# Third feed-forward stage: where the residual is scaled and added, and where the rounding factors lie

## The chip, the cores and the metric

The kernel runs on one core of one Trainium2 chip. The metric is the device time of one execution in microseconds (us); the times shown are medians of several executions. PE is TensorE, DVE is VectorE, ACT is ScalarE, POOL is GpSimd.

## The reference, cut to what matters

A tensor `x` of 64 x 64 x 128 numbers passes through four layers, each a cross attention and a feed-forward. The change lies in the third feed-forward and touches how the fourth attention begins:

```python
x = x + tanh(g_ffn[2]) * L2_ffn(layernorm(x), w_fc, b_fc, w_proj, b_proj)

def block_quant(v, m_bits, bk):          # m_bits 3, bk 32, over the last dimension
    amax = max(abs(vb))                  # of each block of 32
    e = floor(log2(maximum(amax, 2.0 ** -126)))
    scale = exp2(e - m_bits)
    return round(vb / scale) * scale
def lowprec_linear(x, w, b):
    return einsum('bsk,nk->bsn', block_quant(x), block_quant(w)) + b
h = gelu(lowprec_linear(x, w_fc, b_fc))  # hidden width 512
return lowprec_linear(h, w_proj, b_proj)
```

## The kernel before, in words

The 4096 rows of `x` stay in SBUF as 32 tiles of 128 x 128 (`x_sb`). Stages follow one another; the third feed-forward (`ffn2` on each engine) works on pairs of tiles, 16 pairs, in a software pipeline whose order is `pair_order`: `step(c, x, h, px, ph)` for c from 0 to 18, where `x` is the pair whose rows are quantised in step c, `px = c - 1` the pair that passes the first product, `h = c - 2` the pair whose hidden values are quantised, and `ph = c - 3` the pair that passes the second product and gets its residual. Steps 0 and 1 are done inside the attention before. Each engine runs its own queue in program order, and semaphores tie them together.

One step in the middle does this:

- **VectorE** takes the largest magnitude of each block of 32 in one instruction over 128 x 1280 (the rows of one pair and the hidden values of another, L1774), masks out its exponent (an int32 AND in place on `e`, L1777), forms the rounding factor `m = max(e, 2^-126) * 1.5 * 2^20` (L1780), and adds `m` to the numbers (L1781, result `q_r`), which rounds them. Then it adds the residual of pair `ph` (two `scalar_tensor_tensor` of 128 x 128 from PSUM, L1636, called from L1784), measures these tiles for the next normalisation (`bn_stats` L1787, `bn_aggr` L1791), and in every second step adds the epsilon for two pairs (`pair_measured`, L1759, between L1774 and L1777).
- **GpSimd** subtracts the factor again (`lower_blocks`, L1278, 128 x 1280, result `q_out` in bf16), and in every second step takes the power -1/2 of four variances (L1294). From step 16 on it also normalises the first tiles for the next attention (`normal_rows`, L1376 and L1378).
- **TensorE** puts the bias of the first product into PSUM (L641) and the bias of the second (L862), keeps its clock up with two products whose result nobody reads (L522), turns the quantised rows (L638) and hidden values (L897), makes the first product (L881) and the second (L886), and works ahead on keys and values for the fourth attention (L528, L537).
- **ScalarE** copies the turned rows (L1049) and hidden values (L1199) from PSUM, normalises the rows of a later pair (L988), applies Gelu to the first product (L1055), which writes the hidden values into the buffer that VectorE quantises in the next step, and keeps the keys and values that were made ahead (L976, L980).

The Gelu of step c waits for VectorE's addition of the same step, since both use the same buffer:

```python
                if px is not None:
                    act.wait_ge(quotients[0], c + 1)
                    hidden2(px)
```

VectorE's reduction of step c waits for that Gelu of step c - 1 (`hid_ready`). GpSimd's subtraction waits for VectorE's addition (`quotients`), and TensorE's transposes of step c wait for GpSimd's subtraction of step c - 1 (`q_ready`). In the last two steps TensorE issues six and twelve clock-keeping products (L522) ahead of its transposes. The outputs of the second product lie in two PSUM banks, one for each tile of the pair.

## Time and profile before

| | us |
|---|---|
| median of 3 runs (lowest, highest) | 1058.82 (1058.22, 1059.3) |
| the profiled execution | 1061.08 |
| its span, first to last instruction | 1059.3 |
| busy: PE, DVE, ACT, POOL | 896.4, 873.2, 679.0, 577.7 |

The span is the stretch in which instructions ran; 1.78 us of the profiled execution lie around it. The steady steps of the stage lie between about 710 and 768 us of the span, its last three steps end at about 782 us, and the fourth attention follows. A row of a timeline gives the start and the duration of an instruction, or of several alike that follow one another (x2 at its end); the brackets tell how long the engine had been idle before it and what released it.

### The profile page before, as it was taken

How to read it: one execution, taken by the hardware profiler on the slowest of the kernel's cores; microseconds unless marked ns; L12 is line 12 of the kernel's file. 1: busy time of each engine (PE TensorE's matmuls, PEld its weight loads, DVE VectorE, ACT ScalarE, POOL GpSimd, SP SyncE). 2: the span in 40 equal slices, each digit the busy share in tenths (PEclk: the TensorE clock that was granted, in tenths of full speed). 3: DMA queues.
4: the chain of work that ended last, by engine and by line, in shares of the span. 5: the costliest groups of instructions: out<-in, count | busy, mean ns of one | idle time of the engine just before them, and what ended most of it. 6: DMA issues, size and time to landing. Idle time of an engine off the chain costs nothing.

```text
span 1059.3 us, 30026 instructions
## 1 busy us (share of the span) xinstructions
PE 896.4 (85%) x11481; PEld 694.4 (66%) x11481; DVE 873.2 (82%) x2299; ACT 679.0 (64%) x1740; POOL 577.7 (55%) x691
## 2 busy tenths in 40 slices
PE   8999999999999963699959999988889999634553
PEld 5888879988887751366638888844458778412232
DVE  5999988878899974256649999869978999799997
ACT  5888864367777730245438888868867788544553
POOL 6444402243457667322178888235553788667644
PEclk9999999999999976799989999969999999755555
DMA  8760000000000011465311111000000000000000
GB/s 223 177 256 3 2 2 2 2 2 3 3 17 27 28 37 52 123 186 150 103 43 35 32 33 33 7 1 1 2 2 3 2 2 3 1 5 16 15 21 25
DMA packets 60527, 44.43 MB, mean 42 GB/s; under 512 B 15196, under 2 KB 55781, under 8 KB 59366
## 3 DMA queue, kind: packets, MB, share of 16 engines
q1 hardware_dynamic: 55718, 34.09, 11.0%
q0 software_dynamic: 4096, 8.34, 2.7%
q8 instruction: 90, 1.47, 0.6%
q14 instruction: 47, 0.39, 0.1%
q10 hardware_dynamic: 576, 0.13, 0.1%
HBM read 23.73 MB, written 18.87 MB: 40 GB/s over the span
## 4 chain that ended last, share of the span: by engine, by line
PE 53%; DVE 19%; POOL 12%; issue 9%; ACT 3%; DMA 2%; DVEq 1%; POOLq 0%; SPq 0%; ACTq 0%
PE ps L777 8%; PE ps L735 8%; PE ps L708 6%; PE ps L618 4%; POOL big L1248 3%; PE ps L749 3%; PE ps L821 3%; PE ps L812 3%; PE ps L813 3%; PE ps L528 3%; DVE rowmax L1976 2%; POOL slots L1264 2%; PE ps L672 2%; PE ps L628 2%; DVE big L1848 2%
## 5 line engine op out<-in xcount | busy, mean ns | idle before, releaser
L1976 DVE TENSOR_REDUCE rowmax<-ps 128x16 f32<-128x1024 f32 x128 | 155.4, 1214 | 25.8 <-PE ps L708 24.8
L1982 DVE TENSOR_TENSOR sm<-ps,rowmax 128x512 f32<-128x512 f32 x256 | 164.9, 686 | 3.4
L1084 ACT ACTIVATE pr<-ps 128x512 f32<-128x512 f32 x256 | 139.0, 595 | 43.7 <-PE ps L777 39.2
L777 PE MATMUL ps<-cst,sm 128*128 128x128 f32 x1024 | 140.2, 277 | 11.6 <-DVE sm L1982 9.2
L735 PE MATMUL ps<-vbd,pr 128*64 128x18 f32 x4096 | 141.6, 212 | 0.6 <-ACT pr L1084 0.5
L735 PEld LDWEIGHTS ps<-vbd,pr 128*64 128x64 f32 x4096 | 133.9, 138 | 5.2 <-ACT pr L1084 1.6
L777 PEld LDWEIGHTS ps<-cst,sm 128*128 128x128 f32 x1024 | 112.4, 141 | 27.0 <-issue 18.5
L1407 POOL TENSOR_SCALAR xn<-x_sb,mv_all,rstd_all 128x128 f32<-128x128 f32 x122 | 97.5, 799 | 35.7 <-PE ps L672 28.5
L963 ACT ACTIVATE qbd<-ps,bqp,cst 128x128 f32<-128x128 f32 x256 | 104.9, 465 | 5.7 <-PE ps L688 1.9
L1248 POOL DMA_INDIRECT big<-expert_out,row_g x64 | 68.6, 1072 | 38.6 <-DMA expert_out<-xn_all 23.0
L1264 POOL DMA_INDIRECT slots<-xn_all,row_s x64 | 65.0, 1015 | 34.4 <-DVE sm L1982 18.2
L1240 POOL TENSOR_TENSOR rstd_all<-mv_all,cst 128x1 f32<-128x1 f32 x64 | 36.1, 567 | 78.2 <-DVE mv_all L1954 37.8
L908 PE MATMUL ps<-wT,xqT_both 128*128 128x512 bf16 x60 | 28.3, 627 | 56.6 <-ACT xqT_both L1049 54.5
L1021 ACT ACTIVATE vbd<-ps 64x128 f32<-64x128 f32 x192 | 53.4, 278 | 24.2 <-PE ps L528 16.0
L1254 POOL TENSOR_TENSOR rstd_all<-mv_all,cst 128x1 f32<-128x1 f32 x60 | 34.5, 574 | 60.4 <-DVE mv_all L1948 51.0
L1278 POOL TENSOR_TENSOR q_out<-q_r,q_s 128x1280 bf16<-128x1280 f32 (+2 forms) x18 | 37.9, 2105 | 49.8 <-DVE q_r L1781 43.4
L1098 ACT ACTIVATE oT<-ps 128x128 f32<-128x128 f32 x128 | 35.5, 278 | 45.0 <-PE ps L681 44.0
L1636 DVE SCALAR_TENSOR_TENSOR x_sb<-ps,tg,x_sb 128x128 f32<-128x128 f32 x192 | 54.6, 289 | 11.4 <-PE ps L886 7.6
L2095 DVE TENSOR_TENSOR pr<-ps,pr 128x512 f32<-128x512 f32 x32 | 22.0, 691 | 50.4 <-ACT pr L1151 50.2
L749 PE MATMUL ps<-wo,oT 128*128 128x128 f32 x256 | 61.6, 323 | 1.4 <-ACT oT L1098 1.4
L528 PE MATMUL ps<-wv,ctxT 128*64 128x64 f32 x1024 | 53.7, 235 | 2.1 <-ACT big L976 2.0
L1474 POOL TENSOR_TENSOR hid<-sm 128x512 f32<-128x512 f32 x16 | 22.7, 1421 | 59.9 <-DMA sm<-slots 59.9
(314 smaller groups left out, 2356.2 us busy)
## 6 DMA issues: line engine op xcount, KB each, us to landing
slots<-hT SPq DMA_DIRECT2D x8, 1024.0 KB, 11.9
sm<-slots SPq DMA_DIRECT2D x32, 256.0 KB, 3.1
expert_out<-xn_all SPq DMA_DIRECT2D x16, 256.0 KB, 3.0
ew<-in_L_ffn_w SPq DMA_DIRECT2D x24, 128.0 KB, 2.6
out<-x_sb SPq DMA_DIRECT2D x32, 64.0 KB, 1.5
slots<-xn_all,row_s POOLq DMA_INDIRECT x64
big<-expert_out,row_g POOLq DMA_INDIRECT x64, 2.7
x_sb<-in_x SPq DMA_DIRECT2D x1, 512.0 KB, 4.5
```

The lines of the kernel that those rows point to most:

```text
L528: last = nc.tensor.matmul(dst[a * S:(a + 1) * S, b * S:(b + 1) * S].rearrange("p (r w) -> p r w", r=RG), ctxT[:, t * P + b * S:t * P + (b ...
L708: last = nc.tensor.matmul(bank(0, r)[:, b * P:(b + 1) * P], qbd[x][rows, b * S:(b + 1) * S, :].rearrange("d q h -> d (q h)"), keys[rows, : ...
L735: last = nc.tensor.matmul(dst[:, :, h2, :], probs[:, h2, :], heads[:, :, h2, :], start=True, stop=True, skip_group_check=True)
L749: last = nc.tensor.matmul(mixed[:, M_Y], oT[x][:, :], wo[l][:, :], start=True, stop=(l != 2))
L777: last = nc.tensor.transpose(turned[b][:, r * P:(r + 1) * P], sm[x][:, c:c + P], ident)
L963: last = nc.scalar.activation(qbd[y][:, :, a], src[:, P:2 * P], ACT.Identity, scale=parity[:, a:a + 1], bias=bqp[l][:, a:a + 1])
L1084: nc.scalar.activation(pr[y][:, b, :], turned[b], ACT.Exp, scale=SCALE).then_inc(p_ready[y], 1)
L1248: nc.gpsimd.indirect_dma_start(got[i % 2][s][:, k, :], None, eo_d, bass.IndirectOffsetOnAxis(ap=row_g[:, k, t:t + 1].bitcast(U32), axis=0) ...
L1264: nc.gpsimd.indirect_dma_start(slots_d[c], bass.IndirectOffsetOnAxis(ap=row_s[:, c, u:u + 1].bitcast(U32), axis=0), xn_all[:, u * D:(u + 1 ...
L1407: nc.gpsimd.tensor_scalar(xn[buf][:, :], xt, mv_all[:, 2 * u:2 * u + 1], rstd_all[:, u:u + 1], ALU.subtract, ALU.mult).then_inc(xn_ready[b ...
L1976: v.tensor_reduce(row3, sc, AX.X, ALU.max).then_inc(rowmax_ready[x], 1)
L1982: v.tensor_tensor(sm[x][:, :].rearrange("p (r g k) -> p r g k", r=RG, k=S)[:, part], sc[:, part], row3[:, part].unsqueeze(3).broadcast_to( ...
```

## The change

The residual of pairs 0 to 14 no longer goes through VectorE. In the step after the second product, ScalarE multiplies both tiles of the pair by the gate from PSUM into SBUF (`scale_outputs`, the first instruction of its step), and GpSimd adds the result to `x_sb` behind its subtraction of that step (one addition of 128 x 256). VectorE measures the pair one step later than GpSimd adds it, two steps after the product, so `pair_measured` and the power on GpSimd move by two pairs as well. The last pair keeps VectorE's residual; two pairs are measured behind it. Both tiles of the second product now share one bank (`both_y`), and its bias is put there behind the first product instead of ahead of the transposes. From step 2 on VectorE writes the rounding factors into PSUM and reads them there; GpSimd forms its own copy in SBUF from the exponents. VectorE's wait for GpSimd's last subtraction moves from the factor to the addition.

```diff
@@ names, beside the other PSUM views
         outputs = bank(1, 3)[:, P:(1 + NS) * P].rearrange("p (s d) -> p s d", s=NS)
         fp4_ps = bank(1, 2)[:, 0:3 * (HW // Q16)].rearrange("p (n b) -> p n b", n=3)
+        both_y = bank(0, 3)[:, P:(1 + NS) * P]
+        factors = bank(1, 3)[:, 3 * P:3 * P + QMAX // Q32]
+        scaled_y = [hid[p][:, 0:NS * D] for p in range(2)]
+        ADDED = IT - 1
+        BLOCK_STEPS, BLOCK_WEIGHT_STEPS = 3, 4
@@ TensorE, ffn2
                         lift_bias(s)
-                    if ph is not None:
-                        pe.wait_ge(x_done[s], IT * FFN2 + ph)
-                        nc.tensor.matmul(bank(s, 3)[:, P:2 * P], ones_b[0:3, :], bias3[:, F2:F2 + D], start=True, stop=False, skip_group_check=True)
...
                 if ph is not None:
+                    if 1 <= ph <= ADDED:
+                        pe.wait_ge(y_scaled, ph)
                     for s in range(NS):
+                        if ph == 0 or ph > ADDED:
+                            pe.wait_ge(x_done[s], IT * FFN2 + ph)
+                        nc.tensor.matmul(both_y[:, s * D:(s + 1) * D], ones_b[0:3, :], bias3[:, F2:F2 + D], start=True, stop=False, skip_group_check=True)
                         pe.wait_ge(hqT_ready[s], ph + 1)
                         for n in range(4):
-                            last = nc.tensor.matmul(bank(s, 3)[:, P:2 * P], hqT[s][:, n * P:(n + 1) * P], wT[:, 1, n * P:(n + 1) * P],
+                            last = nc.tensor.matmul(both_y[:, s * D:(s + 1) * D], hqT[s][:, n * P:(n + 1) * P], wT[:, 1, n * P:(n + 1) * P],
@@ ScalarE
+            def scale_outputs(i):
+                for s in range(NS):
+                    act.wait_ge(y_ready[s], IT * FFN2 + i + 1)
+                if i > 1:
+                    act.wait_ge(x_done[0], IT * FFN2 + i - 1)
+                nc.scalar.activation(scaled_y[i % 2], both_y, ACT.Copy, scale=tg[:, 6:7]).then_inc(y_scaled, 1)
+
             def ffn2(c, x, h, px, ph):
                 if c < 2:
                     return
+                if ph is not None and 1 <= ph <= ADDED:
+                    scale_outputs(ph - 1)
                 if px is not None:
                     empty_quantised(FFN2, px)
@@ GpSimd, lower_blocks
                     span = both_sides(x, h)
+                    if c > 1:
+                        blk = slice(span.start // Q32, span.stop // Q32)
+                        pool.wait_ge(quant_step[0], BLOCK_WEIGHT_STEPS + BLOCK_STEPS * c + 2)
+                        pool.wait_ge(q_ready[0], c)
+                        nc.gpsimd.tensor_scalar(q_s[:, 1, blk], q_s[:, 0, blk], 2.0 ** -126, 1.5 * 2.0 ** 20, ALU.max, ALU.mult).then_inc(factors_kept, 1)
+                        pool.wait_ge(factors_kept, c - 1)
                     pool.wait_ge(quotients[0], c + 1)
...
                 if c >= IT:
                     normal_rows(3, c - IT)
-                if ph is not None and ph % 2 == 1:
-                    pool.wait_ge(mv_ready[0], IT * FFN2 + ph + 1)
...
+                if ph is not None and 1 <= ph <= ADDED:
+                    xt = x_sb[:, (ph - 1) * NS * D:ph * NS * D]
+                    pool.wait_ge(y_scaled, ph)
+                    nc.gpsimd.tensor_tensor(xt, scaled_y[(ph - 1) % 2], xt, ALU.add).then_inc(x_done[0], 1)
+                    pool.wait_ge(x_done[0], IT * FFN2 + ph)
+                    pool.sem_inc(x_done[1], 1)
+                if ph is not None:
+                    for i in (ph - 2, ph) if ph == IT - 1 else (ph - 2,):
+                        if i > 0 and i % 2 == 1:
+                            pool.wait_ge(mv_ready[0], IT * FFN2 + i + 1)
...
@@ VectorE, ffn2
-                    src, e, m = q_in[:, span], q_s[:, 0, blk], q_s[:, 1, blk]
+                    src, e, m = q_in[:, span], q_s[:, 0, blk], factors[:, blk] if c > 1 else q_s[:, 1, blk]
+                    if c > 2:
+                        dve.wait_ge(factors_kept, c - 2)
                     link(v.tensor_reduce(e, blocks(src, Q32), AX.X, ALU.max, apply_absolute_value=True))
-                    if ph is not None and ph > 0 and ph % 2 == 0:
-                        pair_measured(ph - 1)
+                    if ph is not None and ph > 2 and ph % 2 == 0:
+                        pair_measured(ph - 3)
                     link(v.tensor_scalar(e.bitcast(I32), e.bitcast(I32), EXPONENT, None, ALU.bitwise_and))
-                    if c > 0:
+                    if c == 1:
+                        dve.wait_ge(q_ready[0], 1)
+                    link(v.tensor_scalar(m, e, 2.0 ** -126, 1.5 * 2.0 ** 20, ALU.max, ALU.mult))
+                    if c > 1:
                         dve.wait_ge(q_ready[0], c)
-                    link(v.tensor_scalar(m, e, 2.0 ** -126, 1.5 * 2.0 ** 20, ALU.max, ALU.mult))
                     v.tensor_tensor(blocks(q_r[:, span], Q32), blocks(src, Q32), over(m, Q32), ALU.add).then_inc(quotients[0], 1)
-                if ph is not None:
+                if ph is not None and ph > 1:
+                    measured(ph - 2)
+                if ph == IT - 1:
+                    pair_measured(ph - 2)
                     for s in range(NS):
-                        residual(FFN2, ph, s, tg[:, 6:7], s)
-                    dve.drain()
+                        dve.wait_ge(y_ready[s], IT * FFN2 + ph + 1)
+                        dve.wait_ge(x_done[s], IT * FFN2 + ph)
                     for s in range(NS):
-                        v.bn_stats(bst[s][:, :], x_sb[:, (ph * NS + s) * D:(ph * NS + s + 1) * D])
-                    dve.drain()
-                    for s in range(NS):
-                        u = ph * NS + s
-                        v.bn_aggr(mv_all[:, 2 * u:2 * u + 2], bst[s][:, :]).then_inc(aggr_ready[s], 1)
-                    if ph == IT - 1:
-                        pair_measured(ph)
+                        t = ph * NS + s
+                        xt = x_sb[:, t * D:(t + 1) * D]
+                        v.scalar_tensor_tensor(xt, both_y[:, s * D:(s + 1) * D], tg[:, 6:7], xt, ALU.mult, ALU.add).then_inc(x_done[s], 1)
+                    measured(ph - 1)
+                    measured(ph)
+                    pair_measured(ph)
+
+            def measured(i):
+                for s in range(NS):
+                    dve.wait_ge(x_done[s], IT * FFN2 + i + 1)
+                    dve.wait_ge(aggr_ready[s], IT * FFN2 + i)
+                    v.bn_stats(bst[s][:, :], x_sb[:, (i * NS + s) * D:(i * NS + s + 1) * D])
+                dve.drain()
+                for s in range(NS):
+                    u = i * NS + s
+                    v.bn_aggr(mv_all[:, 2 * u:2 * u + 2], bst[s][:, :]).then_inc(aggr_ready[s], 1)
```

## Rows read from the trace of the kernel before

**Rows 1.** Busy time by stretch: us, each engine busy (instructions), PEclk, DMA, GB/s.

```profile
700.00:709.90 9.90, 8.06 (x61) 5.15 (x62) 4.67 (x10) 5.66 (x12) 3.63 (x2) 0.55 0.00 0
714.75:763.30 48.55, 43.26 (x431) 20.93 (x430) 45.58 (x107) 40.52 (x86) 28.46 (x16) 1.00 0.00 1
```

**Rows 2.** Timeline, two middle steps: start, us, engine, line, operation [idle before <-releaser].

```profile
737.81 2.35 POOL L1278 TENSOR_TENSOR q_out<-q_r,q_s 128x1280 bf16<-128x1280 f32 x1 [0.83 <-DVE q_r L1781]
...
739.07 1.45 DVE L1774 TENSOR_REDUCE q_s<-hT 128x40 f32<-128x1280 f32 x1
...
740.55 0.18 DVE L1777 TENSOR_SCALAR q_s<-q_s 128x40 int32<-128x40 int32 x1
740.60 0.38 ACT L1049 ACTIVATE xqT_both<-ps 128x256 bf16<-128x256 bf16 x1 [0.41 <-PE ps L638]
...
740.99 1.49 DVE L1781 TENSOR_TENSOR q_r<-hT,q_s 128x1280 f32<-128x1280 f32 x1
...
742.40 0.60 DVE L1636 SCALAR_TENSOR_TENSOR x_sb<-ps,tg,x_sb 128x128 f32<-128x128 f32 x2
742.56 2.35 POOL L1278 TENSOR_TENSOR q_out<-q_r,q_s 128x1280 bf16<-128x1280 f32 x1 [2.40 <-DVE q_r L1781]
742.60 1.09 ACT L1055 ACTIVATE hT<-ps 128x512 f32<-128x512 f32 x2
743.09 0.49 DVE L1787 BATCH_NORM_STATS2 bst<-x_sb 128x6 f32<-128x128 f32 x2
...
743.82 1.46 DVE L1774 TENSOR_REDUCE q_s<-hT 128x40 f32<-128x1280 f32 x1
...
745.37 0.17 DVE L1759 TENSOR_SCALAR mv_all<-mv_all 128x4 f32<-128x4 f32 x1
...
745.95 1.49 DVE L1781 TENSOR_TENSOR q_r<-hT,q_s 128x1280 f32<-128x1280 f32 x1
```

**Rows 3.** Timeline around the sixteenth quantisation, GpSimd and VectorE.

```profile
773.06 0.80 POOL L1376 TENSOR_SCALAR xn<-x_sb,mv_all,rstd_all 128x128 f32<-128x128 f32 x1
773.83 0.45 POOL L1378 TENSOR_TENSOR x_sb<-x_sb,y_bias_b 128x128 f32<-128x128 f32 x1
...
774.03 0.28 DVE L1759 TENSOR_SCALAR mv_all<-mv_all 128x4 f32<-128x4 f32 x1
...
774.64 1.23 DVE L1781 TENSOR_TENSOR q_r<-hT,q_s 128x1024 f32<-128x1024 f32 x1
```

**Rows 4.** All instances of two lines: count, duration ns min/median/max, first and last start.

```profile
L1848 DVE SCALAR_TENSOR_TENSOR big<-big x30: 628/684/2186, 928.2 to 1045.7; 128x512 f32<-128x512 f32 x30
...
L1617 DVE TENSOR_SCALAR q_m<-xn_all x1: 952/952/952, 492.7 to 492.7; 128x1536 int32<-128x1536 int32 x1
```

**Rows 5.** Sizes on GpSimd and VectorE: single lines (as rows 4), one group.

```profile
L1428 POOL TENSOR_TENSOR x_sb<-x_sb,y_bias_b x87: 452/458/472, 13.5 to 894.4; 128x128 f32<-128x128 f32 x87
...
L1278 POOL TENSOR_TENSOR big<-big 128x512 f32<-128x512 f32 x30 | 31.1, 1057 | 31.4 <-DVE big L1852 30.5 <-DVE big L1829 0.7
...
L1294 POOL TENSOR_TENSOR rstd_all<-mv_all,cst x8: 1006/1006/1040, 716.5 to 782.9; 128x4 f32<-128x4 f32 x8
...
L1828 DVE TENSOR_SCALAR ps<-big x16: 228/228/228, 922.6 to 1042.7; 128x64 f32<-128x64 f32 x16
```

**Rows 6.** Timeline of ScalarE and VectorE at the start of the steady stretch.

```profile
708.38 1.08 ACT L1055 ACTIVATE hT<-ps 128x512 f32<-128x512 f32 x2
709.80 1.45 ACT L976 ACTIVATE big<-ps,bkp,odd_pair 128x512 f32<-128x512 f32 x2 [0.35 <-PE ps L537]
...
709.94 1.45 DVE L1774 TENSOR_REDUCE q_s<-hT 128x40 f32<-128x1280 f32 x1
```

**Rows 7.** Timeline of the stage's end (columns as rows 2).

```profile
775.95 1.91 POOL L1278 TENSOR_TENSOR q_out<-q_r,q_s 128x1024 bf16<-128x1024 f32 x1 [0.45 <-DVE q_r L1781]
...
780.68 0.84 DVE L1636 SCALAR_TENSOR_TENSOR x_sb<-ps,tg,x_sb 128x128 f32<-128x128 f32 x2 [3.25 <-PE ps L886]
...
782.69 1.23 DVE L1976 TENSOR_REDUCE rowmax<-ps 128x16 f32<-128x1024 f32 x1
```

12 lines of the change are left out of this document (6 added, 6 removed).

## The prediction, made before the changed kernel ran

> **What bounds the kernel now.** I read first the busy time by stretch, to see what the stage of the change is limited by, then the timeline of two middle steps, to find the loop behind that limit, and last the timelines of the stage's two ends. In the steady stretch VectorE is busy 45.58 of 48.55 us, TensorE 43.26, ScalarE 40.52, GpSimd 28.46 [rows 1]. Ten steps fill it, so one takes 4.856 us. VectorE looks like the bound, and the change takes work off it. But the timeline shows three loops of almost the same length [rows 2].
>
> First, VectorE's own queue. From one reduction to the next it is 743.82 - 739.07 = 4.75 us, and 0.21 more where the pair's epsilon is added (745.95 - 743.82 = 2.13 from reduction to addition, against 740.99 - 739.07 = 1.92): 4.75 and 4.96, mean 4.856.
>
> Second, the loop through Gelu. It starts about 0.04 after the addition, takes 1.09, and the reduction can follow by 0.12 (742.60 + 1.09 = 743.69 against 743.82, so 0.12 is an upper bound). Then come 1.92 to the addition and its 1.49: 0.04 + 1.09 + 0.12 + 1.92 + 1.49 = 4.66, with the epsilon 4.87, mean 4.77.
>
> Third, a loop over two steps through GpSimd. Addition's end to subtraction 0.08 (740.99 + 1.49 = 742.48, 742.56); subtraction 2.35; its end to ScalarE's copy 0.44 (737.81 + 2.35 = 740.16, 740.60); copy to Gelu 2.00 (742.60); then 1.09, 0.12, 2.13 and 1.49. Sum 9.70, or 4.85 a step, against 4.856 measured. ScalarE sits idle 0.41 before the copy in this parity, so the lateness comes from GpSimd.
>
> So VectorE, if it lost all that the change removes, would still wait for Gelu, and Gelu for GpSimd.
>
> **What is removed.** VectorE's two residuals go: 743.09 - 742.40 = 0.69 a step [rows 2]. Nothing is late any more on VectorE by itself, and next comes Gelu. By the third loop the gain is at most 4.856 - 4.85, practically 0 a step. The reduction is unchanged; moving the wait for the subtraction from the factor to the addition gains nothing, since the subtraction ends 2.43 after the addition (0.08 + 2.35) and the factor comes later than that. The measuring stays (0.49 and about 0.25) but fits in the 1.25 until Gelu's end. In the first two steps with an output nothing is measured yet.
>
> **ScalarE's scaling.** 128 x 256 from PSUM: a bf16 copy of that width took 0.38, and two Gelus of 512 took 1.09, some 0.55 each [rows 2]; I take 0.42 between 0.38 and 0.55. It comes ahead of the copy, into an idle 0.41 in the tight parity; consecutive instructions of ScalarE overlap by some 0.1 (two of 0.6 in 1.09), so it is just covered: 0, at most 0.1 a step. If this cover were gone, 0.4 a step would go onto the third loop. TensorE's next output product waits for this scaling, but it stands behind the copies that ScalarE does after it. The bias product moves from an idle spell before the transposes into the wait for the copied hidden values: 0.
>
> **Factors in PSUM.** The nearest row that writes PSUM from a small tile is 0.228 for 64 columns [rows 5], against 0.18 for 40 columns in SBUF [rows 2]. I take 0.02 a step, bounds 0 and 0.05. The addition reads one operand from PSUM instead of SBUF; nothing in its 1280 columns changes: 0. GpSimd's own copy of the factors, 128 x 40, is under its 128 x 128 addition of 0.46 [rows 5]; I take 0.35. It runs while VectorE forms the factor and adds (1.7 us), so it is covered, also behind a power of 1.01.
>
> **GpSimd's addition and what it blocks.** This decides the steady part. A two-input addition of 128 columns takes 0.458 and a two-input operation of 512 takes 1.057 [rows 5]; in line, 256 columns take 0.66 (bounds 0.55 and 0.80). It stands right behind the subtraction, so it lasts from 2.43 to 3.08 after VectorE's addition ended. In the same count VectorE's reduction ends at 0.04 + 1.09 + 0.12 + 1.48 = 2.73. The next instruction is the AND in SBUF, or the epsilon. What happens when such a short VectorE instruction meets a GpSimd one shows once: the epsilon at 774.03 took 0.28 instead of the 0.17 of 745.37, and ended at 774.31, while GpSimd's 128 x 128 addition ended at 774.28 [rows 2, 3]. The larger meetings have the same pattern: L1848 has a median of 0.684 and a longest of 2.186 [rows 4]. And the AND is of the kind that runs at two columns a cycle: 1536 int32 columns took 0.952, so 0.62 ns each [rows 4], where the addition takes 1.49 for 1280. So I take it that the AND (or the epsilon) cannot begin until GpSimd's addition has ended, at 3.08, and ends at 3.11.
>
> The Trainium skill has this as a rule ("SBUF — State Buffer", Who interferes with whom): VectorE and GpSimd share a pair of ports that one of them holds for a whole instruction, and a `tensor_scalar` with SBUF on both sides can ask for it. The trace agrees in the 0.28 above. Without the rule the steady part would come out at 0 instead of the +0.4 below. The page "VectorE: DVE Perf Modes" (Why PSUM operands drop a tier) says that a PSUM operand keeps an instruction out of the two-port mode, so by it the factor into PSUM would not be held; no row here shows such a meeting.
>
> The step then goes: AND ends 3.11, factor at 3.15, addition 0.22 + 0.02 later, 1.49: 4.88. With the epsilon: it ends 3.11, the addition starts 774.64 - 774.31 = 0.33 later [rows 3], plus 0.02 and 1.49: 4.95. Mean 4.91, against 4.856: +0.05 a step, over ten steps (from the fourth addition, where the first pair is added, to step 15) +0.5. With a 0.55 addition the third loop holds and this is 0; with 0.80 it is +0.19 a step, +1.9.
>
> **The start.** The reduction at 709.94 came behind residual and measuring; Gelu had ended at 708.38 + 1.08 = 709.46, so it can come 0.36 sooner [rows 6]. But ScalarE was busy until 709.80 + 1.45 = 711.25, and the scaling now stands between that and the copy, without an idle spell: later by 0.3 to 0.4. Of the 0.36 I keep 0.2 as a gain; bounds -0.6 and +0.3.
>
> **The end.** Here GpSimd's queue is the path. Before, its last subtraction started at 775.95 and took 1.91 [rows 7], two normalisations and bias additions followed (0.80 + 0.45 each, less overlap 1.22, as at 773.06 [rows 3]), and it was done by 780.3. VectorE's last residual came at 780.68 and ended at 781.52, and the attention's first row maximum at 782.69 [rows 7], 1.17 later. New: the blocked additions in steps 16 and 17 cost some 0.35; GpSimd then does, from 773.45 on, rows 1.22, an addition 0.66, the power 1.01, the factors 0.35 (776.7), subtraction 1.91 (778.6), rows 1.22, addition 0.66, rows 1.22, addition 0.66: 782.4. VectorE's last residual now waits for that addition, since it needs `x_done` of the pair before. Two tiles take 0.60, and then two pairs are measured instead of one: 1.17 + 0.75 (743.82 - 743.09 = 0.73 [rows 2]). The row maximum comes at 782.4 + 0.1 + 0.6 + 1.9 = 785.0: +2.3. It carries over in full, since the attention's chain of waits runs through that row maximum. TensorE's transposes of the last hidden values (about 778.9) are just not reached by the late subtraction. Bounds: GpSimd on time and only the second measuring, +0.75; everything late, +2.8.
>
> **Sum.** Start -0.2, steady +0.5, end +2.3: +2.6. The profiled execution would go from 1061.08 to 1063.7; it stands 2.26 above the median, so the median goes from 1058.82 to 1061.4.
>
> **Rivals.**
> - *No hold.* The AND goes past GpSimd's addition. Against it the 0.28 [rows 3]; for it that this is one meeting of another operation. Steady 0, and GpSimd's queue at the end loses only the 0.35: -0.2 + 0 + 1.9 = +1.7, 1060.5. Chance 0.15.
> - *The clock falls.* TensorE would be idle from its last output product (about 781) to 783.1 and again for 1.8, where it now waits half a microsecond. In 700 to 709.9 it was granted 0.55 [rows 1], that is, mostly 1.2 GHz instead of 2.4, behind a handover with idle spells. In the fourth attention TensorE is nearly always busy, so an estimate is that 7 us at half clock, less the time it idles anyway, lose some 3: 2.6 + 3.0 = +5.6, 1064.4. Against it: the attention begins with clock-keeping products. Chance 0.2.
> - *Faster.* VectorE's relief shows: Gelu's loop at 4.77 would be the limit if ScalarE came to its Gelu sooner than the third loop says, -0.09 for 13 steps, -1.1; the start gives its whole 0.6; and GpSimd reaches its last addition before TensorE's last output (by 780.7), so that only the second measuring less TensorE's 0.4 from the moved bias is added: +0.35. Sum -1.4, 1057.4. It is decided by GpSimd's last addition: every 0.1 by which it ends after 780.7 goes onto the time. Against it: that sum of queued work ends 1.7 later. Chance 0.1.
> - *The sum above*, with its spread, 0.55.
>
> **The numbers.** About 0.2% (2.1 us) is what a measurement of this kernel can tell from no change. The sum at +2.6 is slower; with its bounds one part in four falls below 2.1. No hold is mostly "same", the clock "slower", the faster rival mostly "same". Slower is 0.55 x 0.75 = 0.41, 0.20 from the clock and 0.01 from no hold, 0.62; the faster rival gives 0.07 to faster and 0.03 to same; the rest is same, 0.31. The range takes from -0.8 (half of the faster rival) to +5.7 (the clock, or long GpSimd additions).
>
> **What would show it.** Steady steps of 4.86 to 4.95, with L1777 or L1759 at 0.4 to 0.5 us instead of 0.18, ending just behind GpSimd's addition. VectorE idle for about 0.5 before each reduction, released by Gelu. The last residual released by GpSimd's addition, and the row maximum 4.3 us behind the last output product instead of 1.5. It is wrong if the steady step falls under 4.8, if the AND stays at 0.18 under a running GpSimd addition, or if the last residual is released by TensorE.

## The result, and the profile after

The changed kernel took 1064.30 us (median of 8 runs, 1062.74 to 1068.29), the kernel before 1058.78 beside it (8 runs, 1057.81 to 1061.27). The ratio is 1.0053, with an interval of 1.0043 to 1.0064: slower by 5.5 us. The profiled execution took 1063.8 us, its span is 1062.0.

To see where the time came from I took the starts of VectorE's reductions in the stage from the timeline, and those of the first row maxima of the attention behind it. "Start" runs from the third reduction to the sixth, "steady" over the ten steps from there, "end" from the sixteenth reduction to the first row maximum, "first step" from there to the second. What lies ahead of the stage and behind it is the same code.

| us | start | steady | end | first step | sum against before |
|---|---|---|---|---|---|
| before | 18.81 | 48.56 | 19.44 | 3.98 | |
| after | 18.99 | 49.98 | 22.39 | 4.70 | +5.3 |

The four stretches together lose 5.3, close to the 5.5 of the timing. They come from one profiled execution each, and outside them the two executions differ where their code doesn't: the one of before reaches the third reduction 2.1 later (695.88 against 693.76) and takes 0.4 longer behind the last stretch, so that the profiled executions as wholes differ by 2.7 only. The steady stretch first, two steps of after in the timeline (columns as [rows 2], where two steps of before stand):

```profile
732.41 1.49 DVE L1806 TENSOR_REDUCE q_s<-hT 128x40 f32<-128x1280 f32 x1 [0.49 <-issue]
733.99 0.41 DVE L1789 TENSOR_SCALAR mv_all<-mv_all 128x4 f32<-128x4 f32 x1
...
734.76 1.49 DVE L1815 TENSOR_TENSOR q_r<-hT,ps 128x1280 f32<-128x1280 f32 x1
...
737.46 1.49 DVE L1806 TENSOR_REDUCE q_s<-hT 128x40 f32<-128x1280 f32 x1 [0.49 <-issue]
738.98 0.48 DVE L1809 TENSOR_SCALAR q_s<-q_s 128x40 int32<-128x40 int32 x1
...
731.24 1.09 ACT L1063 ACTIVATE hT<-ps 128x512 f32<-128x512 f32 x2
...
733.65 0.73 POOL L1318 TENSOR_TENSOR x_sb<-hid,x_sb 128x256 f32<-128x256 f32 x1
...
...
738.69 0.73 POOL L1318 TENSOR_TENSOR x_sb<-hid,x_sb 128x256 f32<-128x256 f32 x1
...
759.00 0.73 POOL L1318 TENSOR_TENSOR x_sb<-hid,x_sb 128x256 f32<-128x256 f32 x1
759.04 0.73 DVE L1809 TENSOR_SCALAR q_s<-q_s 128x40 int32<-128x40 int32 x1
```

VectorE now idles 0.49 before most reductions, as its residuals are gone. The profile names no releaser for it ("issue"), but the reduction starts 0.08 after Gelu's end (731.24 + 1.09 = 732.33, 732.41). GpSimd's addition ends at 733.65 + 0.73 = 734.38 and the epsilon at 734.40; the next one ends at 739.42 and the AND at 739.46. Before, they took 0.17 and 0.18 [rows 2]. So in nine of the ten steps one of the two is held until GpSimd's addition ends, in one of them by only 0.03. A step mostly takes 4.97 from reduction to reduction where the AND is held, 5.04 where the epsilon is, against 4.75 and 4.96. Two of the ten are longer. In the last of the rows above the AND is held for GpSimd's whole addition, since the subtraction ahead of it had started 0.24 later than elsewhere; that step takes 5.22. Another takes 5.18, and the one behind it only 4.86; the experiments come back to it. The first of the ten is a control within the kernel:

```profile
714.28 0.18 DVE L1809 TENSOR_SCALAR q_s<-q_s 128x40 int32<-128x40 int32 x1
...
713.10 0.74 POOL L1318 TENSOR_TENSOR x_sb<-hid,x_sb 128x256 f32<-128x256 f32 x1
```

There GpSimd's addition has ended at 713.84, the AND takes its 0.18, and the step takes 4.67 (712.76 to 717.43).

By groups of the same stretch, GpSimd, VectorE and ScalarE (count, busy us and mean ns of one):

```profile
L1318 POOL TENSOR_TENSOR x_sb<-hid,x_sb 128x256 f32<-128x256 f32 x10 | 7.3, 730 | 0.0
L1184 ACT ACTIVATE hid<-ps,tg 128x256 f32<-128x256 f32 x10 | 4.8, 481 | 0.0
...
L1809 DVE TENSOR_SCALAR q_s<-q_s 128x40 int32<-128x40 int32 x10 | 3.5, 355 | 0.2
L1305 POOL TENSOR_SCALAR q_s<-q_s 128x40 f32<-128x40 f32 x10 | 3.5, 348 | 3.0 <-DVE q_s L1809 2.0 <-POOL rstd_all L1325 1.0
L1812 DVE TENSOR_SCALAR ps<-q_s 128x40 f32<-128x40 f32 x10 | 2.0, 203 | 0.3
L1789 DVE TENSOR_SCALAR mv_all<-mv_all 128x4 f32<-128x4 f32 x4 | 1.4, 356 | 0.4
```

The start, ScalarE and GpSimd in after's timeline. It answers to [rows 6]:

```profile
707.87 1.45 ACT L984 ACTIVATE big<-ps,bkp,odd_pair 128x512 f32<-128x512 f32 x2 [0.92 <-PE ps L543]
709.21 0.47 ACT L1184 ACTIVATE hid<-ps,tg 128x256 f32<-128x256 f32 x1
709.57 0.39 ACT L1057 ACTIVATE xqT_both<-ps 128x256 bf16<-128x256 bf16 x1
...
710.80 2.35 POOL L1295 TENSOR_TENSOR q_out<-q_r,q_s 128x1280 bf16<-128x1280 f32 x1 [1.61 <-PE ps L884]
```

The scaling stands in ScalarE's full queue, the copy behind it is late, and with it TensorE's first product (L884). GpSimd's subtraction, which by the program waits for that product (`h_psum`), idles 1.61 until it, and the next reduction comes 5.72 behind the one before (707.04 to 712.76), where before it was 4.75. The step ahead of that had gained 0.79 (8.60 against 9.39). How much falls to which of the two varies between executions in which this code is the same (8.79 and 5.57, 8.79 and 5.53 in two kernels below), while their sum stays at 14.32 to 14.36, against 14.14 before.

The end, VectorE, GpSimd and TensorE. It answers to [rows 7]:

```profile
782.69 0.61 DVE L1826 SCALAR_TENSOR_TENSOR x_sb<-ps,tg,x_sb 128x128 f32<-128x128 f32 x2 [1.21 <-POOLq L1320]
...
785.13 1.22 DVE L2022 TENSOR_REDUCE rowmax<-ps 128x16 f32<-128x1024 f32 x1
...
779.62 0.72 POOL L1318 TENSOR_TENSOR x_sb<-hid,x_sb 128x256 f32<-128x256 f32 x1
780.61 0.80 POOL L1407 TENSOR_SCALAR xn<-x_sb,mv_all,rstd_all 128x128 f32<-128x128 f32 x1 [0.28 <-POOL x_sb L1318]
...
781.78 0.72 POOL L1318 TENSOR_TENSOR x_sb<-hid,x_sb 128x256 f32<-128x256 f32 x1
...
780.19 0.40 PE L894 MATMUL ps<-wT,hqT 128*128 128x128 bf16 x4
783.40 1.24 PE L714 MATMUL ps<-big,qbd 32*128 32x128 f32 x16 [2.81 <-DVE x_sb L1826]
```

GpSimd is the path here: its last addition ends at 782.50 and releases the last residual, two pairs are measured behind it, and the row maximum follows 2.44 after the residual's start. TensorE is idle for 2.81 meanwhile. What that does to its clock is in the busy time by stretch (columns as [rows 1]):

```profile
781.92:788.75 6.83, 5.35 (x31) 3.75 (x32) 4.63 (x14) 1.60 (x5) 4.79 (x7) 0.50 0.00 0
```

From 781.92 to 788.75 it was granted half, 1.2 GHz, just where the attention begins; the kernel before had the full 2.4 GHz there. The attention's first step took 4.70 instead of 3.98. Its busy time in before and then in after:

```profile
782.69:786.67 3.98, 3.10 (x32) 1.88 (x30) 2.51 (x4) 2.46 (x7) 3.45 (x5) 1.00 0.00 0
```

```profile
785.13:789.82 4.69, 4.69 (x32) 2.99 (x32) 2.51 (x4) 2.46 (x7) 3.44 (x5) 0.61 0.00 0
```

The same 32 products fill the whole step now, where they had left 0.88 of it free.

### The profile page after: what moved, and what is told of

Read it like the earlier page. It is cut to its first block, busy times and chain, and to the rows that moved or that the text cites. A ratio compares the mean times of both kernels' runs of the same rounds, so it can differ in the third digit from the quotient of the medians.

```text
span 1062.0 us, 30107 instructions
## 1 busy us (share of the span) xinstructions
PE 895.1 (84%) x11481; PEld 695.1 (65%) x11481; DVE 868.5 (82%) x2269; ACT 685.1 (65%) x1755; POOL 595.9 (56%) x722
## 4 chain that ended last, share of the span: by engine, by line
PE 53%; DVE 16%; POOL 14%; issue 10%; ACT 4%; DMA 2%; POOLq 0%; SPq 0%; DVEq 0%; ACTq 0%
PE ps L783 9%; PE ps L741 8%; PE ps L714 6%; PE ps L624 4%; POOL big L1265 3%; POOL q_out L1295 3%; PE ps L755 3%; PE ps L827 3%; PE ps L818 3%; PE ps L819 3%; PE ps L534 2%; DVE rowmax L2022 2%; POOL slots L1281 2%; PE ps L678 2%; PE ps L634 2%
## 5 line engine op out<-in xcount | busy, mean ns | idle before, releaser
L916 PEld LDWEIGHTS ps<-wT,xqT_both 128*128 128x128 bf16 x60 | 6.5, 130 | 68.4 <-ACT xqT_both L1057 57.9
```

## The experiments

Twelve kernels, each timed beside the kernel before on its own chip. The profiled executions give the four stretches; the ratio is the timed one. Four of them (AND from PSUM, end repaired, clock kept, bank and factors) ran on a chip where the kernel before takes 1075.45 us; the instructions of the stage take as long there.

| kernel | start | steady | end | first step | sum against before | ratio (interval) |
|---|---|---|---|---|---|---|
| AND from PSUM | 18.73 | 49.19 | 22.24 | 4.82 | +4.2 | 1.0033 (1.0020 to 1.0047) |
| half the addition | 19.02 | 48.90 | 21.40 | 4.19 | +2.7 | 1.0021 (1.0010 to 1.0032) |
| scaling alone | 19.24 | 48.88 | 19.45 | 3.99 | +0.8 | 0.9995 (0.9985 to 1.0005) |
| end repaired | 19.04 | 49.98 | 19.64 | 3.98 | +1.9 | 1.0012 (1.0000 to 1.0024) |
| clock kept | 18.99 | 49.96 | 22.39 | 3.98 | +4.5 | 1.0041 (1.0026 to 1.0056) |
| bank and factors | 19.29 | 49.71 | 19.35 | 3.99 | +1.6 | 1.0009 (0.9996 to 1.0022) |
| bank only | 19.34 | 51.18 | 19.33 | 3.98 | +3.0 | 1.0036 (1.0023 to 1.0049) |
| epsilon later | 19.01 | 57.00 | 24.46 | 3.98 | +13.7 | 1.0113 (1.0098 to 1.0128) |
| epsilon later, end repaired | 19.23 | 57.03 | 22.01 | 3.98 | +11.5 | 1.0118 (1.0103 to 1.0132) |
| epsilon earlier | 18.85 | 55.14 | 22.03 | 3.98 | +9.2 | 1.0059 (1.0044 to 1.0075) |
| the same, rows first | 19.00 | 53.92 | 19.23 | 3.98 | +5.3 | 1.0046 (1.0033 to 1.0059) |
| before, rows first | 18.97 | 48.69 | 19.44 | 3.98 | +0.3 | 1.0007 (0.9998 to 1.0017) |

The ten steady steps are numbered one to ten below.

### The hold: AND from PSUM, and half the addition

```diff
-link(v.tensor_reduce(e, blocks(src, Q32), ...))
+top = tops[:, blk] if c > 1 else e          # tops lies in PSUM
+link(v.tensor_reduce(top, blocks(src, Q32), ...))
-link(v.tensor_scalar(e.bitcast(I32), e.bitcast(I32), EXPONENT, None, ALU.bitwise_and))
+link(v.tensor_scalar(e.bitcast(I32), top.bitcast(I32), EXPONENT, None, ALU.bitwise_and))
```

> The changed kernel, but from step 2 on VectorE's reduction writes the block maxima into PSUM and the AND reads them there (its result still goes to SBUF), so that no form of the AND has SBUF on both sides. Theory (the AND is held by GpSimd's addition): L1777's successor is back from 0.48 to about 0.20 us in every second step although GpSimd's addition is running, the other steps stay held through the epsilon; the ten steady steps go from 49.98 us to about 49.0, the total falls by about 1.0 from 1064.3. Rival (the steady steps are long because ScalarE's scaling delays the copy and Gelu, or because of the PSUM operand of the addition): the AND is shorter, but the steps stay at 49.8 to 50.0 us.

VectorE and GpSimd in its timeline:

```profile
743.62 0.20 DVE L1811 TENSOR_SCALAR q_s<-ps 128x40 int32<-128x40 int32 x1
...
743.32 0.73 POOL L1319 TENSOR_TENSOR x_sb<-hid,x_sb 128x256 f32<-128x256 f32 x1
```

GpSimd's addition runs until 744.05. The AND, which now reads PSUM, begins and ends under it. The steady stretch went from 49.98 to 49.19.

```diff
-nc.gpsimd.tensor_tensor(xt, scaled_y[(ph - 1) % 2], xt, ALU.add)
+nc.gpsimd.tensor_tensor(xt[:, 0:D], scaled_y[(ph - 1) % 2][:, 0:D], xt[:, 0:D], ALU.add)
```

> The kernel after with GpSimd's residual addition cut to 128x128 (0.46 us instead of 0.73); the second tile of each pair doesn't get its residual, the rest is unchanged. Ten steady steps took 48.56 us before and 49.98 after. Hold theory (the AND or epsilon waits until GpSimd's addition has ended): the addition ends 0.27 earlier, about where VectorE's reduction ends, so the AND takes 0.18 to 0.25 again and the ten steps take 49.0 to 49.3 us, as in the kernel whose AND reads PSUM (49.19). Rival, that the addition itself lengthens GpSimd's queue and so the loop through Gelu: it would also help the other kernel's remainder, 48.6 to 48.9. Rival, that the addition's size does not matter: 49.9 to 50.0. End of the stage (last-but-two reduction to first row maximum) 22.39 after: about 0.5 to 0.8 less here, 21.6 to 21.9.

This kernel leaves out the second tile's residual. 48.90 lies on the edge between the hold's range and that of the rival which blames GpSimd's longer queue, so by itself it can't tell them apart, and the end took 21.40, below the 21.6 that I had set as its least; the groups of its steady stretch show that the meeting is gone:

```profile
L1809 DVE TENSOR_SCALAR q_s<-q_s 128x40 int32<-128x40 int32 x10 | 2.0, 198 | 0.2
L1789 DVE TENSOR_SCALAR mv_all<-mv_all 128x4 f32<-128x4 f32 x4 | 0.7, 171 | 0.4
```

The AND is back from 355 ns to 198 and the epsilon from 356 to 171. Of the 1.42 us that after lost in the steady stretch, 0.8 come back in the one way and 1.1 in the other; I take the hold to be that much. It is less than the 2.2 us by which those instructions had grown (3.5 + 1.4 against 2.0 + 0.7), so a second limit stands close behind: both kernels mostly go at 4.86 to 4.90 a step. What it is shows in where Gelu starts. In a step without an epsilon of the kernel with half the addition:

```profile
727.10 2.35 POOL L1295 TENSOR_TENSOR q_out<-q_r,q_s 128x1280 bf16<-128x1280 f32 x1 [0.27 <-POOL q_s L1305]
...
729.89 0.38 ACT L1057 ACTIVATE xqT_both<-ps 128x256 bf16<-128x256 bf16 x1
...
730.17 1.49 DVE L1815 TENSOR_TENSOR q_r<-hT,ps 128x1280 f32<-128x1280 f32 x1
731.89 1.08 ACT L1063 ACTIVATE hT<-ps 128x512 f32<-128x512 f32 x2
```

Gelu starts 0.23 after the addition's end (731.66, 731.89). It comes 2.00 after ScalarE's copy, and the copy 0.44 after the subtraction's end (729.45, 729.89): the same 0.44 and 2.00 as in the prediction's third loop. In the steps with an epsilon Gelu follows the addition by 0.03, and the step is the loop through Gelu with the epsilon in it, 4.86 to 4.87 as the prediction counted it. So VectorE's relief ends at two limits that both lie at what before took on the average, 4.856.

### What remains: ScalarE's scaling

```diff
+if ph is not None and ph >= 1:
+    for s in range(NS):
+        act.wait_ge(x_done[s], IT * FFN2 + ph)
+    nc.scalar.activation(hid[ph % 2][:, 0:NS * D], x_sb[:, (ph - 1) * NS * D:ph * NS * D], ACT.Copy, scale=tg[:, 6:7])
```

> The kernel before, with a 128x256 scaling added on ScalarE ahead of each step's copy (its result goes nowhere); nothing else is moved. Theory that ScalarE's scaling is covered by the idle 0.41 before the copy in the tight parity: ten steady steps 48.5 to 48.7 us as before (48.56). Rival, that it is part of the third loop (GpSimd's subtraction to ScalarE's copy to Gelu): every second step is later by 0.1 to 0.5, ten steps 49.0 to 50.0, and the remainder of 0.63 that the kernel with the AND from PSUM leaves is ScalarE's. At the start (third to sixth reduction, 18.81 before) both expect 0.2 to 0.6 more.

This stand-in reads `x_sb` in SBUF and waits for VectorE's residual; it takes 0.54, not 0.48. Put into the kernel before, it costs 0.32 in the steady stretch and 0.43 at the start. Neither range had the 0.32. Of the ten steps nine are as before within 0.04, so there the scaling is covered. One, the sixth, takes 5.02 where it was 4.75:

```profile
741.49 0.28 PE L638 MATMUL ps<-ident_b,q_out 128*128 128x128 bf16 x2 [0.33 <-POOL q_out L1282]
...
742.16 0.38 ACT L1049 ACTIVATE xqT_both<-ps 128x256 bf16<-128x256 bf16 x1 [0.30 <-issue]
```

ScalarE's copy starts 0.39 after the transposes' end there, and 0.10 in every other step; the profile names nothing that it waits for. All nine kernels with a scaling ahead of that copy have this gap in the sixth step and in no other of the ten (0.39, in three of them 0.55), and the three with neither the scaling nor another order on ScalarE have 0.10 in all ten. What it is stays open. It is the 5.18 of after, where the next step gives 0.18 of it back, since the addition then just misses the epsilon, and most of what the kernel with half the addition has over before (0.34). In the changed kernel the scaling so costs next to nothing net in the steady stretch. The timing (0.5 us faster, 1.6 faster to 0.5 slower) doesn't confirm the 0.8 of the profiled executions, so a cost of this size is read from the trace, not timed.

### The end and the clock

```diff
 # GpSimd, per step
-if c >= IT:
-    normal_rows(3, c - IT)
 (the addition of the pair before)
+if c in (IT - 3, IT - 1, IT + 2):
+    normal_rows(3, {IT - 3: 0, IT - 1: 1, IT + 2: 2}[c])
 # VectorE, last step
 pair_measured(ph - 2)
+measured(ph - 1)
 (waits for output and x_done, last residual)
-measured(ph - 1)
 measured(ph)
```

> The changed kernel with another order at the end alone: GpSimd normalises the attention's tiles 0 and 1 in steps 13 and 15, and tile 2 behind its last addition, and VectorE measures pair 14 ahead of its wait for the last output. Theory (the end is GpSimd's queue plus the second measuring): from the last full reduction (step 15) to the attention's first row maximum 22.4 us becomes 19.7 to 20.4, and the total falls by 2 to 2.7 from 1064.3; the last residual is released by TensorE again. In steps 13 to 15 the AND or the epsilon may be held once more, up to +0.5. Rival (the end is long through TensorE, its clock or its transposes): 22 us or more stays, total 1064.

VectorE and GpSimd at the end of it:

```profile
796.66 0.61 DVE L1827 SCALAR_TENSOR_TENSOR x_sb<-ps,tg,x_sb 128x128 f32<-128x128 f32 x2
...
798.26 1.23 DVE L2022 TENSOR_REDUCE rowmax<-ps 128x16 f32<-128x1024 f32 x1
...
793.98 0.72 POOL L1316 TENSOR_TENSOR x_sb<-hid,x_sb 128x256 f32<-128x256 f32 x1
794.88 0.73 POOL L1316 TENSOR_TENSOR x_sb<-hid,x_sb 128x256 f32<-128x256 f32 x1 [0.17 <-ACT hid L1184]
```

GpSimd's last addition now ends at 795.61, one microsecond ahead of the residual, and only one pair is measured behind it (1.60 from residual to row maximum instead of 2.44). The residual waits for nobody: VectorE comes to it straight from measuring the pair before, not released by TensorE as I had expected. The end takes 19.64, just under the 19.7 to 20.4 and 2.75 less than after, and the clock doesn't fall, which brings 0.72 more. That is 3.5 us of the 5.3; the ratio falls from 1.0053 to 1.0012.

```diff
 pair_order(pe, ffn2)
+pe.wait_ge(ahead_kept, 2 * GROUPS)
+keep_clock(12)
 attention(3)
```

> The changed kernel plus twelve clock-keeping products on TensorE between its last output product and the attention's first scores. Theory (the wait there costs the clock, and the clock costs about 0.7 us): the granted clock stays 1.0 at 782 to 789, the second row maximum follows the first after 4.0 us instead of 4.69, the total falls by 0.5 to 1.0 from 1064.3, everything ahead of the first row maximum stays. Rival (the clock costs the 3 us of the prediction's estimate): the total falls by 2 or more. Other rival (it falls for another cause): no difference in granted clock.

Busy time by stretch of this kernel, up to the first row maximum and the attention's first step behind it:

```profile
781.00:803.20 22.20, 20.54 (x178) 10.99 (x178) 14.25 (x42) 13.98 (x31) 18.43 (x21) 1.00 0.01 1
803.22:807.20 3.98, 2.44 (x28) 1.58 (x27) 2.52 (x4) 1.81 (x5) 3.43 (x5) 1.00 0.00 0
```

With products in TensorE's gap the clock stays at full and the first step takes 3.98, while the end stays 22.39. So the fallen clock cost 0.72 us, by the trace; the two ratios, 1.0053 and 1.0041, have intervals that overlap. Until the first row maximum TensorE's slow products cost nothing.

### Both outputs in one bank, and the factors in PSUM

First the kernel after without its scaling and without GpSimd's addition: VectorE adds and measures every pair in its own step as before, out of the one bank, and the factors stay in PSUM with GpSimd's copy beside them.

```diff
-scale_outputs(ph - 1)                                # ScalarE
-nc.gpsimd.tensor_tensor(xt, scaled_y[...], xt, ALU.add)
-measured(ph - 2)                                     # VectorE
+v.scalar_tensor_tensor(xt, both_y[:, s * D:(s + 1) * D], tg[:, 6:7], xt, ALU.mult, ALU.add).then_inc(x_done[s], 1)
+measured(ph)
```

Then the kernel before with the bank alone, in which VectorE also waits for both outputs before its first residual:

```diff
-pe.wait_ge(x_done[s], IT * FFN2 + ph)                 # early in the step, one bank for each s
-nc.tensor.matmul(bank(s, 3)[:, P:2 * P], ones_b[0:3, :], bias3[:, F2:F2 + D], start=True, ...)
 ...
+for s in range(NS):                                   # behind the first product
+    pe.wait_ge(x_done[s], IT * FFN2 + ph)
+for s in range(NS):
+    nc.tensor.matmul(both_y[:, s * D:(s + 1) * D], ones_b[0:3, :], bias3[:, F2:F2 + D], start=True, ...)
```

> Of the change only the bank shared by both outputs with the bias behind the first product, and the factors in PSUM with GpSimd's own copy; the residual of every pair is VectorE's as before, and no scaling and no addition on GpSimd. Theory (these parts are nearly free): ten steady steps 48.6 to 49.0 us against 48.56 before, the end 19.2 to 19.6 against 19.44, the total 1058.5 to 1059.5. Rival (the PSUM factors or the shared bank carry part of the loss): steady steps above 49.5.

> The kernel before, with both outputs in one bank and the bias product moved behind the first product, in front of the output's own; factors, residual and everything else as before. It splits the kernel that had one bank and the factors in PSUM (ten steady steps 49.71 us against 48.56 before). Theory that the later bias and the wait for both outputs make VectorE's residual late in every second step: 49.1 to 49.7 here. Rival, that the factors in PSUM and GpSimd's factor copy cost it: 48.5 to 48.8 here.

My first expectation was a miss: 49.71, and not 48.6 to 49.0. VectorE's timeline of that kernel:

```profile
755.66 1.49 DVE L1803 TENSOR_TENSOR q_r<-hT,ps 128x1280 f32<-128x1280 f32 x1
757.52 0.61 DVE L1810 SCALAR_TENSOR_TENSOR x_sb<-ps,tg,x_sb 128x128 f32<-128x128 f32 x2 [0.38 <-PE ps L892]
```

The addition ends at 757.15 and the residual waits 0.38 for the output product. That is so in the steps without an epsilon, which take 5.08 instead of 4.75; those with one take 4.86 instead of 4.96 (from the fourth step on). The kernel with the bank alone loses no less: eight of its steps have a mean of 5.02. So the bank, the later bias and the wait for both outputs together cost 0.12 to 0.16 a step on the average where the residual is added in the same step, and some 0.5 at the start (19.29 and 19.34 against 18.81); for a cost of the factors in PSUM nothing is left. One thing does go with the factors: GpSimd starts its subtraction 0.13 to 0.14 after VectorE's addition in this kernel and in after, and 0.08 in before and with the bank alone. In the changed kernel I take the bank's cost to be hidden, since nobody needs the output before the next step; no run here changes the bank alone in it. The 51.18 also holds two long steps, 5.28 and 5.75, 1.0 above the others. What made the first I don't know; in the second TensorE was granted half:

```profile
730.45:733.87 3.42, 3.42 (x42) 2.46 (x42) 2.35 (x7) 2.32 (x6) 2.23 (x1) 0.50 0.00 0
```

### Three places for the epsilon

The epsilon is added between reduction and AND, in the loop through Gelu. I tried to take it off. First behind the step's addition:

```diff
-if ph is not None and ph > 2 and ph % 2 == 0:       # between reduction and AND
-    pair_measured(ph - 3)
 v.tensor_tensor(... over(m, Q32), ALU.add).then_inc(quotients[0], 1)
+if ph is not None and ph > 2 and ph % 2 == 0:
+    pair_measured(ph - 3)
```

> The kernel after, whose reduction leaves the block maxima in PSUM so that the AND reads them there (as in the earlier run, 49.19 for ten steady steps), and whose pair epsilon stands behind the step's addition instead of between reduction and AND. Theory that what remains of 0.63 over before is the epsilon still held in every second step (0.41 instead of 0.17) and its place on the chain: ten steps 48.3 to 48.7. Rival, that the remainder is the longer third loop (scaling on ScalarE, factor copy on GpSimd): 49.0 to 49.2, since the epsilon is then in slack.

> All three repairs of the changed kernel together: AND from PSUM, epsilon behind the addition, and the end with the normal rows of the first tiles earlier and one pair measured ahead of the last wait (the run of that alone: end 19.64 us instead of 22.39, first attention step 3.98 instead of 4.70, ratio 1.0012). If the costs are independent they add: steady 48.3 to 48.7, end 19.6 to 19.7, clock kept, start 18.9 to 19.1; in sum 0.0 to +0.4 us against before, ratio 0.9995 to 1.0005. If the remainder of the steady part belongs to the third loop: steady 49.0 to 49.2, ratio 1.0003 to 1.0010.

Both were far off: 57.00 and 57.03 instead of 48.3 to 49.2. GpSimd in the timeline of the first, in a step at full clock:

```profile
762.82 1.03 POOL L1326 TENSOR_TENSOR rstd_all<-mv_all,cst 128x4 f32<-128x4 f32 x1 [2.16 <-DVE mv_all L1790]
...
764.54 2.35 POOL L1296 TENSOR_TENSOR q_out<-q_r,q_s 128x1280 bf16<-128x1280 f32 x1
```

The power stands in GpSimd's queue ahead of the factor copy and the subtraction. It now waits 2.16 for the epsilon, and the subtraction starts 1.94 after VectorE's addition has ended (761.11 + 1.49 = 762.60), where it had started 0.13 after it. The next reduction waits for the factor copy too, 1.20. Such a step takes 5.47 and the one behind it 5.92. A part of the 57.00 is not the queue's alone: TensorE was granted half from 731.3 to 741.6 and again for some 3 us from 755 on, 0.87 in the mean of the ten steps in both kernels, and the longest step, 7.21, lies there. I had looked at who waits for the epsilon, and not at what is queued behind the one who waits. The second time the epsilon went forward, right behind the pair's measuring, into VectorE's idle time:

```diff
 if ph is not None and ph > 1:
     measured(ph - 2)
+    if ph % 2 == 1:
+        pair_measured(ph - 2)
```

> The changed kernel with the AND reading PSUM, the end repaired (normal rows earlier, one pair measured ahead of the last wait), and the pair's epsilon moved forward, right behind that pair's measuring into VectorE's idle time ahead of the next reduction (the run that moved it back behind the addition was 8 us slower over ten steps, because GpSimd's power waits for it ahead of its factor copy and subtraction). Theory that in the kernel with the AND from PSUM (49.19) every second step was limited by GpSimd's queue (subtraction, addition, power, factor copy: 5.09 from subtraction to subtraction) together with the epsilon on VectorE's chain: 48.2 to 48.9. Rival, that the epsilon is in slack: 49.1 to 49.2. Rival, that it was all the chain: 47.5 to 48.0. End as in the run of that repair alone, 19.4 to 19.7, first attention step 3.98. In sum -0.2 to +0.6 us against before.

55.14, a miss again, and for another reason. VectorE and GpSimd:

```profile
746.31 2.01 DVE L1790 TENSOR_SCALAR mv_all<-mv_all 128x4 f32<-128x4 f32 x1
748.23 1.48 DVE L1808 TENSOR_REDUCE ps<-hT 128x40 f32<-128x1280 f32 x1
...
745.95 2.35 POOL L1296 TENSOR_TENSOR q_out<-q_r,q_s 128x1280 bf16<-128x1280 f32 x1 [1.82 <-PE ps L885]
```

That idle time lies under GpSimd's subtraction. An epsilon on four columns, 0.17 when nothing meets it, took 2.01 and ended at 748.32, as the subtraction ended at 748.30; elsewhere it took 1.65 or 1.66, and a step 5.91. It is the clearest row for the hold in the whole study. TensorE's clock was at half for 10 us within the ten steps and for 7 more at the end, and the end took 22.03. That the late steps made it fall isn't shown: the next kernel has steps of 5.91 as well, and its clock stayed full:

```profile
731.97:742.20 10.23, 9.86 (x70) 5.81 (x72) 7.83 (x15) 6.84 (x15) 6.47 (x6) 0.50 0.01 2
```

### The loop through GpSimd and ScalarE

```diff
+if c + 1 < IT:
+    rows2(c + 1)
 if px is not None:
     empty_quantised(FFN2, px)
 ...
-if c + 1 < IT:
-    rows2(c + 1)
```

> The same kernel, with ScalarE's two normalised rows of the next step moved ahead of its copy of the transposed input, into the idle time in which it waits for TensorE's transposes; Gelu then comes 0.9 us sooner behind that copy. Theory that the loop through GpSimd's subtraction, ScalarE's copy and Gelu holds the steps once VectorE's queue has been relieved: ten steps 47.4 to 48.2 us. Rival, that GpSimd's own queue or VectorE's chain through Gelu holds them: no less than the kernel without this move. In sum against before -1.2 to -0.3 us if the theory holds.

> The kernel before with only that move of the two normalised rows ahead of the copy. Theory that before VectorE's own queue (4.856 a step) is the bound and the loop through GpSimd just its equal: ten steps 48.3 to 48.6 us, no change that the timing could show. Rival, that the loop through GpSimd is the true bound of before: 47.7 or less, and then the change's relief of VectorE was not needed for the gain.

The steady stretch took 53.92, so the range was missed: this kernel still has the early epsilon. Where that is out of the way one sees what the loop allows:

```profile
734.11 1.48 DVE L1808 TENSOR_REDUCE ps<-hT 128x40 f32<-128x1280 f32 x1
...
738.79 1.49 DVE L1808 TENSOR_REDUCE ps<-hT 128x40 f32<-128x1280 f32 x1 [0.49 <-issue]
```

4.68 for the step without an epsilon: its Gelu follows 0.02 behind VectorE's addition, so that is the loop through Gelu alone. But the kernel without this move has steps of 4.68 too. The move does what it was meant to where ScalarE had come late: in most of the steps in which Gelu had started 0.22 or 0.23 after the addition, it starts 0.03 after it. No gain shows, since the reduction behind is held up by the early epsilon. Of the three steps of 6.2 to 6.3 in the kernel without the move one lies within the stretch at half clock and one begins at its end. So the 1.2 us between the two kernels may be the clock's, and what the rows' place is worth is not shown. The control is clear: in the kernel before, the same move gives 48.69 against 48.56, 0.1 above the range that I had given, and a ratio of 1.0007. There VectorE's own queue was the bound, as read.

Not tried was the combination that these runs point to: the epsilon where the change has it, the AND from PSUM, the end repaired, with and without the rows first. Without them, the stretches measured one by one would be 18.9, 49.19, 19.64 and 3.98, by that estimate 0.9 us above before. No kernel in this study beat the one before.

## Why the prediction was right, and where it was off

The time forecast was 1061.4, slower than 1058.82; it came to 1064.30. The loss, 5.5, is over twice the 2.6 of the sum, and it lies 0.2 inside a range that had been drawn as wide for a fallen clock priced four times too high. So the range held in part by luck. The direction and the mechanisms of the hold and of the end held, the three terms of the sum were too small, and one rival came true beside it.

- **VectorE's residuals bring nothing.** Right. VectorE idles 0.49 until Gelu has ended, and even without the hold the 0.69 of work taken off left steps of 4.86 to 4.90, no shorter than 4.856. The two loops that the prediction had counted behind VectorE's queue are what holds them, Gelu's with the epsilon in one parity and GpSimd's in the other.
- **The hold.** Right as a mechanism, shown by rows of four kernels: gone with a PSUM operand, gone with an addition half as long, and 2.01 us long where the same epsilon meets the subtraction. Mis-sized: for a 128 x 256 addition I took 0.66 in line between 0.458 and 1.057; it took 0.73. GpSimd also started its subtraction 0.13 to 0.14 after VectorE's addition, not 0.08. The addition so ended 3.17 after VectorE's, not 3.08, and a step took 4.97 and 5.04, not 4.88 and 4.95. (The +0.4 in the paragraph on the rule is a slip for the +0.5 of the sum. The faster rival's 0.6 at the start has no row behind it; the rows gave 0.36.)
- **Steady part.** Forecast +0.5, measured +1.42. The 0.09 in each of nine steps makes 0.8. The late subtraction of the step of 5.22 adds 0.24, and the first step, 4.67 without a hold, takes as much off. GpSimd's copy of the factors had been counted as covered behind a power too; in that step it wasn't. The scaling, costed at nothing, took 0.48, not 0.42, and cost nothing but the gap in the sixth step, 0.2 less the 0.18 of the next.
- **Start.** Forecast -0.2, measured +0.18. The gain came (0.79 in one step), and more went in the next. I had seen that the scaling stands in a full queue there, but not that GpSimd's subtraction waits for the product that the late copy feeds. Alone the scaling cost 0.43 there; I had named 0.3 to 0.4 and set more gain against it than there was.
- **End.** Forecast +2.3, measured +2.95, by the mechanism given: GpSimd's queue releases the last residual, and two pairs are measured behind it; the row maximum comes 4.5 behind the last output product, and I had said 4.3. I had left out the 0.24 to 0.28 for which GpSimd idles wherever it waits for its own previous result (780.61 above), three times in this chain. Since the stage came 0.5 earlier by then, the row maximum at 785.13 fell on my 785.0 only by chance.
- **The clock falls.** A rival at 0.2, and it happened, in the place named, behind the 2.81 for which TensorE idled; the second idle spell that I had expected is filled by clock-keeping products. Its price was wrong: I wrote 3 us, it was 0.72. In the seven microseconds at half clock TensorE is busy 5.35. But what it does before the first row maximum holds nobody up, and of the first step 2.3 go to five clock-keeping products (L528) whose result nobody reads: they took 1.24 at full clock, and the 1.1 more went mostly into the 0.88 that was free. That the rival's 1064.4 is so near the result is no merit; it came by other terms.
- **Small edits.** The factor in PSUM took 0.203 instead of 0.18 to 0.20, GpSimd's copy 0.348 against 0.35 taken. That the moved bias costs nothing in this kernel is taken, not shown; with the shared bank it cost 0.12 to 0.16 a step where the output is used in the same step.

On the hold the Trainium skill ("SBUF — State Buffer", Who interferes with whom) says that the one who issues first keeps the shared pair of ports for its whole instruction. The rows agree, from 0.48 under an addition to 2.01 under a subtraction. The Trainium skill ("VectorE: DVE Perf Modes", Why PSUM operands drop a tier) says that a PSUM operand keeps an instruction out of the mode that takes both read ports; the AND of 0.20 that ran through under GpSimd's addition agrees, with 0.79 us for ten steps.

## What to carry to other kernels

Work moved from a full engine to an idle one pays no more than the distance to the next limit. Here VectorE's queue did set the step, at 4.856, and 0.69 less of it brought nothing, since two loops stood right behind; work out the longest loop without the removed work before anything else. Whatever goes to GpSimd with both sides in SBUF can stop a tiny VectorE instruction for nearly its own whole length, so ask what VectorE issues in that window, and let that read PSUM if it can. And at a stage's end read the helper's queue by itself, with a quarter of a microsecond for each of its own waits: work that a steady step hides comes out there, and 2.95 of these 5.5 us did.

## What was not expected of the hardware

- The length of the hold has no relation to the work held: 128 x 4 elements, 0.17 us, became 2.01. And not every instruction of VectorE is held: in after `bn_aggr` at 731.68 took its usual 0.25 wholly under GpSimd's subtraction (731.34 to 733.69), and the reduction at 732.41 took its 1.49.
- GpSimd needs 0.24 to 0.28 us between an instruction and the next that waits for its result.
- ScalarE's copy came 0.39 instead of 0.10 after the transposes in the same one step of ten, in every kernel in which a scaling stands ahead of it, with nothing in the profile that it waited for.
- TensorE's clock fell to half in the middle of a steady stretch in four kernels, and stayed down for 3.4 us in one and 10.2 in another. One step took 5.75 meanwhile, among others of 5.02. Late steps alone don't make it fall: with steps of 5.91 it stayed full in one kernel. What does isn't shown.
